# Attention by query block and pair: smaller stacks, maxima of two heads in one reduce, the causal mask of the maxima by a matmul

## The reference

```python
q = (h @ Wq.T + bq).reshape(B, S, nh, hd)      # B = 1, S = 2048, nh = 16, hd = 16
k = (h @ Wk.T + bk).reshape(B, S, nh, hd)
v = (h @ Wv.T + bv).reshape(B, S, nh, hd)
scores = jnp.einsum('bqhd,bkhd->bhqk', q, k) * scale
scores = jnp.where(causal, scores, jnp.finfo(scores.dtype).min)
attn = jax.nn.softmax(scores, axis=-1)
o = jnp.einsum('bhqk,bkhd->bqhd', attn, v).reshape(B, S, H)
return o @ Wo.T + bo
```

## Time and profile before

| | |
|---|---|
| median of 3 runs | 1346.52 us (1343.22 to 1347.28) |
| profiled execution | 1343.12 us, its span 1341.4 us |
| instructions | 23100 |
| TensorE matmul busy | 1144.6 us, 85% of the span |
| VectorE busy | 936.7 us, 70% |
| ScalarE busy | 644.9 us, 48% |
| GpSimd busy | 89.1 us, 7% |
| attention | 434.1 to 997.1 us of the span |

### The profile page before, as it was taken

The page is one execution under the profiler, slowest core; times in us unless marked ns, Lnnn a source line. Parts: engine busy times, 40 slices in busy tenths (PEclk is TensorE's granted clock), DMA queues, the critical chain, the costliest instruction groups (busy, mean ns, idle before and its releaser), DMA issues. The chain is left out here.

```text
span 1341.4 us, 23100 instructions
## 1 busy us (share of the span) xinstructions
PE 1144.6 (85%) x6456; PEld 723.5 (54%) x6456; DVE 936.7 (70%) x1997; ACT 644.9 (48%) x1206; POOL 89.1 (7%) x282
## 2 busy tenths in 40 slices
PE   3289998999785197999999899999876999979997
PEld 2178886888664012233333333333225788868886
DVE  7857776777766496877878587878016677757776
ACT  6434343444355004666666566666762343434443
POOL 0000000000000001021111111120221000000000
PEclk9999999999988557999999999999988999989999
DMA  5000000000036212020201010100000000000000
GB/s 162 1 1 1 1 1 0 0 0 0 5 98 177 76 34 56 1 57 2 56 11 48 16 44 28 30 2 1 2 12 0 1 1 17 1 18 1 4 13 17
DMA packets 57076, 33.51 MB, mean 25 GB/s; under 512 B 38272, under 2 KB 53888, under 8 KB 56960
## 3 DMA queue, kind: packets, MB, share of 16 engines
q1 hardware_dynamic: 56960, 32.12, 8.8%
HBM read 21.43 MB, written 10.49 MB: 24 GB/s over the span
## 5 line engine op out<-in xcount | busy, mean ns | idle before, releaser
L909 ACT ACTIVATE attn_prob<-psum 128x512 f32<-128x512 f32 (+3 forms) x640 | 301.6, 541 | 154.5 <-PE psum L809 150.6
L294 PE MATMUL psum<-ffn_xt,all_w_hi 128*128 128x512 f32 x1024 | 330.9, 405 | 18.8 <-DVE ffn_act_out L425 11.5
L816 PE MATMUL psum<-attn_stack 96*128 96x512 bf16 (+3 forms) x640 | 228.1, 379 | 58.1 <-DMA attn_vals<-v_rows 38.0
L940 DVE TENSOR_REDUCE attn_part_max<-psum 128x1 f32<-128x512 f32 x384 | 240.8, 683 | 24.7 <-PE psum L816 23.2
L809 PE MATMUL psum<-attn_stack 99*128 99x512 bf16 (+3 forms) x640 | 211.5, 356 | 20.5 <-ACT attn_prob L909 13.5
L294 PEld LDWEIGHTS psum<-ffn_xt,all_w_hi 128*128 128x128 f32 x1024 | 188.4, 193 | 59.1 <-DVE ffn_act_out L425 13.6
L308 PE MATMUL psum<-all_w_hi,ffn_inner 128*128 128x256 f32 x1024 | 203.3, 281 | 15.0 <-DVE ffn_inner L386 10.4
L294 PE MATMUL psum<-ffn_xt,all_w_lo 128*128 128x512 f32 x512 | 206.1, 403 | 0.0
L944 DVE CUSTOM_DVE_ANT_0 attn_junk<-psum,attn_mask 128x128 bf16<-128x128 f32 (+3 forms) x256 | 118.4, 487 | 87.3 <-PE psum L816 79.7
L308 PEld LDWEIGHTS psum<-all_w_hi,ffn_inner 128*128 128x128 f32 x1024 | 165.3, 188 | 23.2 <-DVE ffn_inner L386 12.0
L353 ACT ACTIVATE ffn_arg<-psum 128x512 f32<-128x512 f32 x128 | 76.6, 598 | 206.9 <-PE psum L294 206.9
(11 more groups left out here) (102 smaller groups left out, 909.5 us busy)
## 6 DMA issues: line engine op xcount, KB each, us to landing
qk_parts<-qkv_parts SPq DMA_DIRECT2D x16, 384.0 KB, 2.6
attn_stack<-qk_parts SPq DMA_DIRECT2D x32, 192.0 KB
attn_stack<-qk_parts SPq DMA_DIRECT2D x32, 128.0 KB
all_x<-in_L_attn_h SPq DMA_DIRECT2D x4, 512.0 KB, 7.6
v_rows<-qkv_rows_v SPq DMA_DIRECT2D x16, 128.0 KB, 3.4
attn_stack<-qk_parts SPq DMA_DIRECT2D x32, 64.0 KB
attn_vals<-v_rows SPq DMA_DIRECT2D x8, 256.0 KB
out<-all_x SPq DMA_DIRECT2D x4, 512.0 KB, 3.0
```

Source lines behind the costliest of these rows:

```text
L294: last = nc.tensor.matmul(psum[:, 2 * m + q % 2, :], w_part[a][:, 3 * g + m, pl, o:o + P], xt[:, k, c, pl, :], start=(n == 0), stop=(n == 5))
L816: nc.tensor.matmul(psum[:, M0 + (b * NM + 2 * m + hd) % MBANKS, 0:cols], q_of(b, hd)[0:KR, i * P:(i + 1) * P], k_of(b, hd)[0:KR, c * BT:c ...
L909: nc.scalar.activation(prob[:, n % PRING, at:BT], psum[:, S0 + (j * NT + n) % SBANKS, at:BT], ACT.Exp).then_inc(s["exp"], 1)
L940: nc.vector.tensor_reduce(to, psum[:, bank, :], AX.X, ALU.max).then_inc(s["max_read"], 1)
```

## The change

The order of the loops is turned: the outer one goes over the four query blocks, the inner one over the eight pairs. A group is one query block of one pair, 32 in all, with 2, 4, 6 or 8 steps; the 160 steps themselves are the same. No hardware loop is left, every instruction stands in the stream once.

A group's stack holds 512 columns of queries and as many columns of keys as the block needs. There are four buffers (`SB`) in place of three. A load has 13 DMAs as before, with shorter rows, and there are 32 loads in place of 8. SyncE issues four of them first. Load g waits until the last step of group g-4 is weighed.

Maxima of both heads go to two neighbouring banks, and one reduce reads both. There are two such slots, and `turn_max` and `gather` use them too. On the diagonal a matmul of `tri` with the identity adds the mask into the bank, and the custom operation is gone. `chunk_steps` places the chunks: no later than 4 steps before their group begins, at most 4, 3 or 2 chunks to a step, and no earlier than two steps after group g-3 begins. With its numbers groups 0 and 1 come before the first step; groups 2 to 7 have their four chunks in steps 0, 2, 4, 6, 8 and 10; group 8 has its eight in step 12, group 9 in steps 14 to 16, group 10 in steps 18 to 20; steps 49 to 148 have two chunks each, and the last 11 none. The splitting of the maxima goes from VectorE to GpSimd and happens for each group, `turn_max` comes two chunks after a group's last one, and VectorE copies the turned rows in place of ScalarE. GpSimd sets the constant rows of the keys by a memset of 32 x 16,384 elements.

```diff
-SB = 3
+SB = 4
 SBANKS = 3
-MBANKS = 3
+MSLOTS = 2
...
-            steps = [(qt, kb) for qt in range(NB) for kb in range(0, SUB * (qt + 1), 2)]
+            groups = [(qt, p) for qt in range(NB) for p in range(NPAIR)]
+            NG_A = len(groups)
+            steps = [(g, kb) for g, (qt, _) in enumerate(groups) for kb in range(0, SUB * (qt + 1), 2)]
...
+            chunks = [(g, i, c) for g, (qt, _) in enumerate(groups) for i in range(SUB) for c in range(qt + 1)]
+            AHEAD = 3
+            def chunk_steps():
+                room = [4 if d < 14 else 3 if d < 48 else 2 for d in range(NS)]
+                at, d = [], NS - 1
+                for g, _, _ in reversed(chunks):
+                    loaded = begin[g - SB + 1] + 2 if g >= SB else -1
+                    d = min(d, begin[g] - 1 - AHEAD)
+                    while d > loaded and not room[d]:
+                        d -= 1
+                    d = max(d, loaded)
...
+                        def load(g):
+                            qt, p = groups[g]
+                            b = g % SB
+                            if g >= SB:
+                                sp.wait_ge(s["weighted"], begin[g - SB + 1])
+                            keys = (qt + 1) * BT
...
+                        for g in range(SB):
+                            load(g)
+                        for d in range(-1, NS):
+                            for e, a in enumerate(chunk_at):
+                                if a == d and closed(e) is not None:
+                                    max_row(closed(e))
+                            if d == chunk_at[-1]:
+                                max_row(NG_A - 1)
+                            if d >= 1 and ended(d - 1) is not None and ended(d - 1) + SB < NG_A:
+                                load(ended(d - 1) + SB)
...
+                        nc.gpsimd.memset(k_st[KR:P, :, :, :], -1.0).then_inc(s["made"], 1)
...
+                        for d in range(-1, NS):
+                            for e, a in enumerate(chunk_at):
+                                if a == d and e in ends:
+                                    split_max(ends.index(e))
+                            for j in range(4):
+                                if (d, j) in masks:
+                                    mask(d, j)
...
+                        def maxima(e):
+                            g, i, c = chunks[e]
+                            qt, b = groups[g][0], g % SB
+                            if i == 0 and c == 0:
+                                pe.wait_ge(s[f"stack{b}"], 13 * 16 * (g // SB + 1))
+                            bank = m_bank()
+                            cols = BT if c < qt else P * (i + 1)
+                            for h in range(2):
+                                last = nc.tensor.matmul(psum[:, bank + h, 0:cols], q_st[0:KR, b, h, i * P:(i + 1) * P],
+                                                        k_st[0:KR, b, h, c * BT:c * BT + cols], start=True, stop=(c < qt))
+                                if c == qt:
+                                    last = nc.tensor.matmul(psum[:, bank + h, cols - P:cols], tri[:, :], identb[:, :], start=False, stop=True)
+                            last.then_inc(s["m_full"], 1)
...
+                        def turn_max(g):
+                            pe.wait_ge(s["max_parts"], g + 1)
+                            bank = m_bank()
...
+                            nc.vector.tensor_reduce(part_max[:, g % 2, :, i, c], psum[:, bank:bank + 2, 0:cols], AX.X, ALU.max
+                                                    ).then_inc(s["m_free"], 1)
```

More of the change, by code:

```diff
@@ L879, in _ @@
-                        pe.wait_ge(s["stack0"], loaded(0, 0))
-                        for m in range(len(chunks)):
-                            for hd in range(2):
-                                maxima(0, 0, m, hd)
-                        pe.wait_ge(s["ones"], 4)
-                        turn_max(0)
-                        pe.wait_ge(s["mask"], 12)
-                        loop(nc.tensor, pair)
-                        weigh(NPAIR - 1, (NPAIR - 1) % SB, NS - 1)
-                        gather(NPAIR - 1, NB - 1, 0)
+                            last.then_inc(s["m_full"], 1)
@@ new lines, in _ @@
+                        pe.wait_ge(s["made"], 4)
+                        for e, a in enumerate(chunk_at):
+                            if a < 0:
+                                maxima(e)
+                                if closed(e) is not None:
+                                    turn_max(closed(e))
+                        pe.wait_ge(s["made"], 15)
+                        for d in range(NS):
+                            for j in range(4):
+                                score(d, j)
+                                for e in chunks_of(d, j):
+                                    maxima(e)
+                                    if closed(e) is not None:
+                                        turn_max(closed(e))
+                                if j == 1 and d == chunk_at[-1] + 1:
+                                    turn_max(NG_A - 1)
+                                if j == 2 and d >= 2 and ended(d - 2) is not None:
+                                    gather(ended(d - 2))
+                            if d >= 1:
+                                weigh(d - 1)
@@ new lines, in _ @@
+                        for d, (g, kb) in enumerate(steps):
+                            if d >= 2:
+                                act.wait_ge(s["weighted"], d - 1)
+                            for j in range(4):
+                                at = first_query(groups[g][0], kb + j // 2)
+                                n = 4 * d + j
+                                act.wait_ge(s["scored"], n + 1)
+                                nc.scalar.activation(prob[:, n % PRING, at:BT], psum[:, S0 + n % SBANKS, at:BT],
+                                                     ACT.Exp).then_inc(s["exp"], 1)
+                            if d >= 1 and ended(d - 1) is not None:
+                                copy_out(ended(d - 1))
@@ L991, in _ @@
-                        dve.sem_inc(s["max_read"], MBANKS)
-                        dve.sem_inc(s["gathered"], CREDIT)
-                        dve.sem_inc(s["normed"], 1)
-                        for b in range(SB):
-                            last = nc.vector.memset(stack[KR:P, b, :, 1, :], -1.0)
-                        last.then_inc(s["ones"], 1)
-                        dve.sem_inc(s["weighted"], CREDIT)
-                        dve.wait_ge(s["mask"], 12)
-                        for m in range(len(chunks)):
-                            for hd in range(2):
-                                maxima(0, 0, m, hd)
```

410 lines of the change are left out of this document (181 added, 229 removed).

## The result

The changed kernel takes 1455.3 us (median of 4 runs, 1454.5 to 1459.1) against 1345.5 beside it: a ratio of 1.082, 95% interval 1.080 to 1.085. The direction was forecast, the size was not: 1375 was predicted, with 1334 to 1403 as the range. The profiled execution has a span of 1457.1 us.

What follows compares the result with a forecast made beforehand. TensorE's stream was taken to set the pace when VectorE's maxima keep up. Block 0 and waits to 592.8 us, groups 8 to 31 433, tail 3: 1028.8 against 997.1, +31.7 on 1343.1, so 1375; range 1334 to 1403.

Steps and rivals of the forecast that it cites:

- Start: Stage start: four loads of 8.4 us issue before the first row of maxima; first score 470.9 against 511.1, gain 40.2 us.
- A round of block 0: Groups 4 to 7: TensorE waits for each load; issue 8.4, landing 2.1, rest of step 5.5, in all 16.0 us.
- End of block 0: Groups 8 and 9 load 12.3 us each, compute 7.5 and 3.0; with steps 15 and 18 the end is 592.8.
- Blocks 1 and 2: Groups of four and six steps, from TensorE's time with loads costing nothing: 13.0 and 17.9 us each.
- Slots: Gather and turn need one of two slots whose reduce is running: about 0.5 us a group, bounds 0 and 1.0.
- Block 3: Groups of eight steps: 23.7 us each, weigh to weigh 2.86 us.
- Masking matmul and reduce: Maxima: 0.1 us a masking matmul, bounds 0.05 and 0.15; two-bank reduce 1.2 us, so VectorE saves little.
- (a): Early rounds: the clock holds at the high level, 17 us less, 1358; chance 0.19 together with (b).
- (b): Early loads: short rows issue at the floor of 6.1 us a load, 1354; chance 0.19 together with (a).
- (d): Turn chain stalls on row maximum and four GpSimd operations; 24 groups lose 36 us, 1411; chance 0.18.
- (c): Masking matmuls and turns vanish in waits, slots never block; three groups cost 49.5 instead of 54.6 us, 1334; chance 0.13.
- (e): Loads never bind, since prefetch is four deep; 70 us are not lost, 1305; chance 0.05.

Runs made afterwards that it cites:

- Run 12: Changed kernel with one-bank slots, reordered stack copies, rows of maxima on ScalarE's queue, and stack copies permitted once the group four before is scored: 1312.1 us.
- Runs 1 and 2: Changed kernel with, in 1, stack copies reordered to 16 rows outermost: 1407.5 us; in 2, rows of maxima issued from ScalarE's queue: 1413.5 us.
- run 8: Changed kernel with only the first four stacks loaded, and four one-bank slots with one reduce per head and chunk: 1312.8 us, output not attention's.
- run 4: Changed kernel with only the first four stacks loaded, with all keys and 16 rows outermost, 28 loads left out: 1371.5 us, output not attention's.
- run 6: Kernel before the change with only the causal mask done by a matmul and a plain maximum on VectorE: ratio 0.9996.
- two transfer edits: Changed kernel with stack copies reordered to 16 rows outermost and rows of maxima on ScalarE's queue: 1393.6 us; with one-bank slots too, 1348.0 us.

## Why the prediction was wrong

- **Start.** Right. The load took 8.1 us to issue (8.4 forecast), the first score came at 470.08 (470.9). GpSimd's memset took 13.7 us (16.8 estimated) and was covered. The fit that the prediction cites from the Trainium skill's page "DMA: Bandwidth & Descriptors" stands there for DMAs that GpSimd issues, and these are SyncE's; the sum doesn't rest on it.
- **A round of block 0.** Right: 16.0 forecast, 16.2 to 16.5 measured, at a clock of 0.54. One round in the timeline of the changed kernel:
```profile
504.20 1.91 SPq L747 DMA_DIRECT2D attn_q_st<-qk_parts  x3
...
511.93 0.42 SPq L753 DMA_DIRECT2D attn_vals<-v_rows  x1
514.30 0.11 PEld L865 LDWEIGHTS psum<-attn_k_st,attn_q_st 96*128 96x128 bf16 x1 [5.37 <-DMA attn_vals<-v_rows]
...
516.86 1.53 SPq L760 DMA_DIRECT2D attn_q_st<-attn_max_rows  x2
```
  Issue, landing and the rest of the step follow each other: 8.1, 2.0 and 6.1 us where I had 8.4, 2.1 and 5.5. Run 12 showed why they do: the weigh that permits a load stands behind the maxima that wait for the load before.
- **End of block 0.** The copies of groups 5, 6 and 7 come at 576.8, 594.1 and 605.9 where I had 571.2, 586.5 and 592.8: the two longer loads took 12.9 and 13.0 us (12.3 forecast), which is the small part. TensorE's work behind the first of them took 11.0 us for 7.5, behind the second 4.3 for 3.0, and steps 15 and 16 took 11.8 us at a clock of 0.55 without a DMA wait, where the sum has 3.3 for step 15 and 3 for a wait.
- **Blocks 1 and 2: the step that failed.** I took 13.0 and 17.9 us a group and let the loads cost nothing after step 18. Measured: 19.2 and 21.2. Two causes, each shown. First, the row of maxima waits in SyncE's queue behind 8 us of issue and on the DMA engines behind copies that use one to three of them; I had priced a row's issue and landing (1.5 and 1.6 us) for the first row only and put it at nothing for the other 31. Runs 1 and 2 each remove 30 us of block 1, together 40; with no later loads block 1 is 40 us shorter and block 2 9. Second, the slots: without later loads they cost 11 us in block 1 and 23 in block 2.
- **Slots: a term mis-sized.** I took 0.5 us a group, bounds 0 and 1.0; 8 against 4 gives 1.8, 58 us in all. In block 2 the turn and the gather fall into one step, wait 1.45 us, and the clock falls behind them; I had no term for that. (The 13.0 of block 1 is 11.7 and 1.3, so the slot term is missing from it.) Without the slot term my sums hold: 13.0, 17.4 and, with the 4 us for the last steps off, 22.7 us a group against the 12.9, 17.2 and 21.9 of run 8.
- **Block 3.** Close, in part by luck: 23.9 us for its full groups where 23.7 was forecast, but the slots cost 1.1 us a group there for 0.5, and the rest came out 0.8 under my sum; the weighs from 932.26 to 940.90 are 2.84 to 2.95 apart as in the earlier trace rows.
- **Masking matmul and reduce.** Within their bounds. The matmul's start costs 0.06 us at full clock (0.1 forecast, bounds 0.05 and 0.15), the reduce of two full banks 1.22; run 6 shows that mask and plain maximum together make no difference.
- **The rivals.** (a) and (b) did not come: the clock was 0.54 in block 0, and a load takes 8.1 us to issue with its short rows. (d), the turn chain, came nearest in size (1411), but not in its mechanism: GpSimd's four operations take 0.19 to 0.20 us each, about 1.0 with gaps, and TensorE's matmuls wait 1.5 us for them in all 32 turns, 3.8 in run 8, where no slot holds the turn. (c) supposed slots that never block, and runs 4 and 8 refute that; even in run 8 its three groups take 52.0 us (12.1, 17.3 and 22.5), not 49.5. (e), loads that never bind, would have given about 1371 and not 1305, by run 4, as the slots stood behind them.

The gains don't add. One-bank slots are worth 15 us with the loads in place, 46 when two transfer edits are there, and 59 without loads. The end-to-end loss of 110 us comes from four costs that overlap: the load permission, which acts in block 0, the copies' width and the queue of the rows, which both act most in block 1, and the slots, which act in every block and most in block 2. ScalarE's two issues add 0.7 us to a group of block 3 with two-bank slots (23.9 to 24.6) and 1.2 with one-bank slots (22.5 to 23.7); waits of 0.48 and 1.00 us for an exponential are the larger part of it. Not settled: how the cost of the slots divides between their number and their size, and why a row's two DMAs take up to 9.9 us on the queue behind long copies. The rows on a third queue, GpSimd's, were not tried.

## What to carry to other kernels

When an in-order queue carries both bulk loads and a small row that a matmul needs at once, price the row behind the load, on the queue and on the engines. Trace what permits a prefetch: if the permission stands behind a wait for the prefetch before, several buffers work like one. Joining two banks into one operation saves VectorE little (1.22 for 2 x 0.63 us), and with two such slots each small job waits for a whole long reduce, in front of everything behind it. Price such a wait with the clock: here the lower clock behind the waits cost as much as the waits.

## What the runs showed of the hardware

- The order of a copy's dimensions alone was worth 48 us in the changed kernel and 14 in the kernel before, at equal bytes and equal count of DMAs.
- Three DMAs of a stack mostly cost SyncE's queue 1.87 us, with the outermost dimension of 16 1.82, and the rows' length changes nothing: 512, 1024 or 2048 keys.
- Two DMAs of 3 KB spent 1.54 us on the queue right behind a load of 1024 keys, and 3.9 to 9.9 us within 3 us of one of 1536 or 2048 keys (changed kernel). With the order of run 1 it was 2.0 or less everywhere behind block 0.
- Idle times of 0.54 and 0.91 us with a matmul of 0.22 between them were followed by a granted clock of 0.57 in the 4 us behind the next scores; with 0.26 us of idle in the same place it stayed at 1.00.
- A masking matmul of 128 columns, accumulated onto a bank that was just written, has a mean duration of 0.26 us, but the next matmul starts 0.06 us after it at full clock (571.16 and 571.22 in run 4).
